# A twelve-stage decoder on one core: the order tables of four engines laid anew for all sixteen batches, with some of the PSUM banks they take

## The chip, the core and the metric

The kernel runs on one core of one Trainium2 chip. Its engines are TensorE (PE, matrix products), VectorE (DVE), ScalarE (ACT) and GpSimd (POOL); SyncE (SP) issues the DMAs. Each works through its own list of instructions in order and waits on semaphores that the others raise. The metric is the device time of one execution in microseconds (us), lower is better.

## What is computed

64 sequences of 128 tokens with 128 channels pass twelve sub-layers; each is added to its input and normalized:

```python
x = _layernorm(x + _L0_attn_ref(x, ...), axis=-1)                        # rec
x = _layernorm(x + _L0_xattn_ref(ctx_1024, x, ctx_1024, ...), axis=-1)   # x0
x = _layernorm(x + _L0_ffn_ref(x, ...), axis=-1)                         # f0, 8 routed experts
x = _layernorm(x + _L1_attn_ref(x, ...), axis=-1)                        # a1
x = _layernorm(x + _L1_xattn_ref(x, ctx_1024, ...), axis=-1)             # x1
x = _layernorm(x + _L1_ffn_ref(x, ...), axis=-1)                         # f1, fp4 rounding
x = _layernorm(x + _L2_attn_ref(x, ...), axis=-1)                        # a2
x = _layernorm(x + _L2_xattn_ref(x, ctx_1024, ...), axis=-1)             # x2
x = _layernorm(x + _L2_ffn_ref(x, ...), axis=-1)                         # f2, 6 low-rank experts
x = _layernorm(x + _L3_attn_ref(x, ...), axis=-1)                        # a3
x = _layernorm(x + _L3_xattn_ref(x, ctx_1024, ...), axis=-1)             # x3
x = _layernorm(x + _L3_ffn_ref(x, ...), axis=-1)                         # f3, attention, then 8 gated experts
return x
```

(The comments are the kernel's names of the stages.) Everything is float32. Most attentions have 16 heads of 8 channels, over 128 tokens or over a context of 77.

## The kernel before

**Opening.** Up to about 466 us the kernel prepares weights and solves the recurrence of the first layer (`opening`). It has its own table, `MEMORY_ORDER`, which the change leaves alone.

**Batches and groups.** The decoder then treats the sequences as 16 batches of four (`SEQS = 4`), called batch 0 to 15 here. Three groups (`GROUPS = 3`) each own a set of SBUF tiles, and group n works through the batches n, n+3, n+6 and so on: group 0 has six of them, the last being batch 15; group 1 ends with batch 13 and group 2 with batch 14. So three batches at different stages are in flight most of the time, and batch 15 is alone at the end.

**Steps.** For each engine a generator (`whole_tensor`, `whole_scalar`, `whole_vector`, `whole_gpsimd`) issues a batch's work in steps, one for each `yield`: 329 steps a batch on PE, 255 on ACT, 548 on DVE, 27 on POOL. The steps of one batch always come in the same order on an engine (`BATCH` lists their names). Each step ends by raising its group's semaphore, and a step that needs another engine's result waits for that semaphore's value.

**What sets the order between groups.** `ORDER` holds a string of digits for each engine: which group takes its next step. `in_order` turns it into the one list of instructions of the engine:

```python
def in_order(programs, order):

    for who in order:
        next(programs[who], None)
```

Since an engine's list is strictly in order, a step that must wait holds up everything behind it, of all groups. What hides the wait is what the table puts ahead of the waiting step.

**An attention stage** (`attention_tensor`, `attention_scalar`, `attention_vector`; x0, x1, a2, x2, a3, f3) goes through the four sequences n in a chain between engines: PE "scores n" (L1533, 16 matmuls of 32 rows), DVE four "top" reductions (L1625), PE "tops turned" (L1545), DVE "q shifted" (L1628), PE "shifted n" (L1559, 32 rows of the trace), ACT four exponentials "p n r" (L1612), and only then PE "scores n+1", since it overwrites the same banks. "out n-1" (L1582), "by tokens n-2" (L1593) and DVE's "o n-2" (L1646) follow with a lag; "shifted n" waits for "o n-2".

**The gated experts** of f3 (`gated_tensor`, `gated_scalar`, `gated_vector`) are 32 "hidden" steps (L2657, one 128x512 product), each evicted by ACT or DVE in turn (L2685, L2697), and 32 steps of an expert's second product (L2672, four 128x128 products; an expert has four), with DVE adding the result (L2704). They need only weights, so they make 64 dense steps a batch. After them come two normalizations and the store (`end_vector`, `store_sync`).

**Banks.** The eight PSUM banks are four pairs. `GIVEN` lists, as digits two by two, which group takes its next stage's pair and which pair (`give_banks`, `take_banks`); a stage's first step on PE waits for the last read by the stage that had the pair before.

**DMAs.** SP has a table of its own (`ORDER["sync"]`), which stays as it is. In it the store of batch 14 stands after the first four of the 16 weight pieces that batch 15's experts need, and ahead of the other twelve; SP waits there for batch 14's last normalization (`end normal`).

## Time and profile before

| | us |
|---|---|
| median of 3 runs | 5805.88 |
| the runs | 5800.32 to 5806.29 |
| span of the profiled execution | 5796.4 |
| PE busy in it | 4942.6 |
| DVE busy | 3559.6 |
| ACT busy | 2315.6 |
| POOL busy | 706.1 |

The profiled execution's span, from its first to its last instruction, is 9.5 us below the median of the runs, which is measured around the execution. A time of the changed kernel is therefore its span plus 9.5.
### The profile page before, as it was taken

The page shows a single profiled execution, that of the slowest core. Times are in us where ns is not written, and L with a number is a line of the kernel's source. Part 1 is how long each engine was busy: PE and PEld are TensorE (multiplying, and loading weights), DVE is VectorE, ACT ScalarE, POOL GpSimd, SP SyncE. Part 2 cuts the span into 40 slices and gives each one's busy share as a digit, 9 for nine tenths or more (in the row PEclk, how much of TensorE's full clock was granted, in tenths as well). Part 3 has the DMA queues.
Part 4 walks back from the last instruction along what each step waited for, and adds up shares of the span by engine and source line. Part 5 has one row for each costly group of instructions (what it writes and reads, how often), then busy time and mean ns, then how long its engine had stood idle before and what let it go on. Part 6 is the DMA issues. An engine that isn't in the chain of part 4 may idle for free.

```text
span 5796.4 us, 130530 instructions
## 1 busy us (share of the span) xinstructions
PE 4942.6 (85%) x55217; PEld 3576.2 (62%) x55217; DVE 3559.6 (61%) x9609; ACT 2315.6 (40%) x4634; POOL 706.1 (12%) x738
## 2 busy tenths in 40 slices
PE   5655888899898889988889989889898988988787
PEld 3544666567665666766656666666666666665554
DVE  7572576655666665657576666656656666656552
ACT  3111444434434444444543443444434344343331
POOL 6361001101101001100000110100110010110000
PEclk7576899899999999999999999999999989998897
DMA  1113000012020001110000111000020000010000
GB/s 58 25 41 100 30 13 19 3 37 61 12 63 9 23 14 32 62 39 30 31 2 28 39 41 54 16 30 18 23 67 31 30 28 13 30 41 23 1 30 26
DMA packets 144930, 184.57 MB, mean 32 GB/s; under 512 B 46074, under 2 KB 73826, under 8 KB 143714
## 3 DMA queue, kind: packets, MB, share of 16 engines
q1 hardware_dynamic: 144354, 176.23, 9.9%
q8 instruction: 442, 7.24, 0.5%
q14 instruction: 134, 1.10, 0.1%
HBM read 164.32 MB, written 11.57 MB: 30 GB/s over the span
## 4 chain that ended last, share of the span: by engine, by line
PE 69%; DVE 12%; ACT 6%; issue 3%; DMA 1%; POOL 1%; SPq 0%; POOLq 0%; DVEq 0%; ACTq 0%
PE g_bank L2672 8%; PE g_bank L2657 8%; PE g_bank L1559 7%; PE g_bank L1533 6%; PE g_bank L1582 6%; ACT g_keys_exps L1612 4%; DVE g_tops L1625 3%; PE g_bank L1503 2%; PE g_bank L2395 2%; PE g_bank L1909 2%; PE g_bank L1434 2%; PE g_bank L1919 2%; PE g_bank L1389 1%; PE g_bank L2002 1%; PE g_bank L1593 1%
## 5 line engine op out<-in xcount | busy, mean ns | idle before, releaser
L1625 DVE TENSOR_REDUCE g_tops<-g_bank 128x4 f32<-128x512 f32 (+1 forms) x1536 | 813.8, 575 | 431.1 <-PE g_bank L1533 429.5
L1612 ACT ACTIVATE g_keys_exps<-g_bank 128x512 f32<-128x512 f32 (+1 forms) x1536 | 801.7, 596 | 690.6 <-PE g_bank L1559 689.2
L1368 POOL TENSOR_TENSOR g_rstd<-g_rstd,minus_half 128x4 f32<-128x4 f32 x224 | 226.7, 1013 | 4358.1 <-DVE g_rstd L1350 4340.2
L2672 PEld LDWEIGHTS g_bank<-region,g_keys_exps 128*128 128x128 f32 x4096 | 516.9, 192 | 159.6 <-issue 144.6
L2657 PE MATMUL g_bank<-g_xT,region 128*128 128x512 f32 x1024 | 554.0, 623 | 15.3 <-DVE g_keys_exps L2697 8.4
L2672 PE MATMUL g_bank<-region,g_keys_exps 128*128 128x128 f32 x4096 | 547.4, 278 | 10.8 <-DVE g_base L2704 9.8
L1559 PE MATMUL g_bank<-g_qa,g_keys_exps 32*77 32x128 f32 (+1 forms) x12288 | 490.8, 300 | 74.4 <-DVE g_o L1646 38.3
L1559 PEld LDWEIGHTS g_bank<-g_qa,g_keys_exps 32*77 32x77 f32 (+1 forms) x12288 | 408.8, 181 | 191.7 <-issue 62.6
L1533 PE MATMUL g_bank<-g_keys_exps,g_qa 32*128 32x154 f32 (+1 forms) x6144 | 411.6, 381 | 100.3 <-ACT g_keys_exps L1612 91.9
L1582 PE MATMUL g_bank<-g_keys_exps,g_v 77*32 77x128 f32 (+1 forms) x12288 | 444.4, 289 | 60.7 <-DVE g_tops L1625 50.9
L1582 PEld LDWEIGHTS g_bank<-g_keys_exps,g_v 77*32 77x32 f32 (+1 forms) x12288 | 333.4, 115 | 176.8 <-DVE g_tops L1625 117.7
L1533 PEld LDWEIGHTS g_bank<-g_keys_exps,g_qa 32*128 32x128 f32 x6144 | 275.5, 198 | 212.3 <-ACT g_keys_exps L1612 125.3
L1606 ACT ACTIVATE g_oT_sc<-g_bank 128x256 f32<-128x256 f32 x384 | 147.5, 384 | 541.5 <-PE g_bank L1582 540.9
L2685 ACT ACTIVATE g_keys_exps<-g_bank,region 128x512 f32<-128x512 f32 x256 | 175.9, 687 | 469.0 <-PE g_bank L2657 468.7
L2697 DVE TENSOR_SCALAR g_keys_exps<-g_bank,region 128x512 f32<-128x512 f32 x256 | 191.3, 747 | 277.0 <-PE g_bank L2657 276.0
L1628 DVE TENSOR_TENSOR g_qa<-g_qa,g_bank 128x256 f32<-128x256 f32 x384 | 159.4, 415 | 189.2 <-PE g_bank L1545 186.8
L1377 ACT ACTIVATE g_x<-g_x,g_shift,g_rstd 128x128 f32<-128x128 f32 x384 | 171.4, 488 | 201.5 <-DVE g_shift L1354 201.2
L2657 PEld LDWEIGHTS g_bank<-g_xT,region 128*128 128x128 f32 x1024 | 159.5, 193 | 73.0 <-issue 61.1
L1593 PE MATMUL g_bank<-consts_sb,g_oT_sc 128*128 128x128 f32 x768 | 165.4, 300 | 30.5 <-ACT g_keys_exps L1612 17.1
L2704 DVE SCALAR_TENSOR_TENSOR g_base<-g_bank,g_gates,g_base 128x128 f32<-128x128 f32 x512 | 149.9, 341 | 53.3 <-PE g_bank L2672 46.9
L1343 DVE BATCH_NORM_STATS2 g_stats<-g_x 128x6 f32<-128x128 f32 x768 | 176.0, 279 | 3.7
L1545 PE MATMUL g_bank<-consts_sb,g_tops 128*128 128x128 f32 x384 | 119.1, 310 | 66.8 <-DVE g_tops L1625 65.7
(376 smaller groups left out, 8832.0 us busy)
## 6 DMA issues: line engine op xcount, KB each, us to landing
region<-L_w_in SPq DMA_DIRECT2D x512, 256.0 KB, 2.9
region<-xT_in SPq DMA_DIRECT2D x16, 256.0 KB, 2.7
z_scratch<-m_uT SPq DMA_DIRECT2D x1, 4096.0 KB, 11.0
g_oT_sc<-z_scratch SPq DMA_DIRECT2D x16, 256.0 KB, 3.2
g_xT<-xT_in SPq DMA_DIRECT2D x16, 256.0 KB, 3.9
g_o<-x_in SPq DMA_DIRECT2D x16, 256.0 KB, 4.1
out<-g_x SPq DMA_DIRECT2D x16, 256.0 KB, 2.3
region<-weights_in SPq DMA_DIRECT2D x1, 3020.5 KB, 10.1
```

Of the source, the lines that this page charges most:

```text
L1343: e.bn_stats(g.stats[:, n, :], src[:, n, :]).then_inc(*b.vector(f"{st} stats {n}"))
L1368: e.tensor_tensor(g.rstd[:, :], g.rstd[:, :], g.s["minus_half"], ALU.pow).then_inc(*b.gpsimd(st + " rstd"))
L1533: ins = e.matmul(bank[r][:, 2 * nk * t:2 * nk * (t + 1)].rearrange("p (i k) -> p i k", i=2), g.qa[rows, t, n, :], g.km[rows, n, t, :, 0:nk ...
L1559: ins = e.matmul(bank[r][0:nk, u * T:(u + 1) * T], g.km[rows, n, t, i, 0:nk], g.qa[rows, t, n, :], start=not masked, stop=not masked or u ...
L1582: ins = e.matmul(b.bank[st][0][32 * u:32 * u + 32, k * T:(k + 1) * T], g.v[0:nk, n, 8 * i + 4 * k + u, :], g.p[0:nk, 2 * i + k, u, :], sta ...
L1593: ins = e.transpose(b.bank[st][1][:, k * P:(k + 1) * P], outputs_of(g, n)[:, k, :], g.k["ident"])
L1612: e.activation(g.p[0:nk, r, :, :], bank[r][0:nk, :].rearrange("p (u q) -> p u q", u=4), ACT.Exp, scale=scale).then_inc(*b.scalar(f"{st} p ...
L1625: e.tensor_reduce(g.tops[:, first:first + 4].rearrange("p (t i) -> p t i", t=2), src, AX, ALU.max).then_inc(*b.vector(f"{st} top {n} {r}"))
L2657: e.matmul(bank[0][:, :], weights.part(f"w1 {x}", c), g.xT, start=True, stop=True).then_inc(*b.tensor(f"f3 hidden {k}"))
L2672: ins = e.matmul(bank[1][:, n * D:(n + 1) * D], g.gated_hid[:, x % 2, c, n * T:(n + 1) * T], weights.part(f"w2 {x}", c), start=c == n == 0 ...
L2685: e.activation(g.gated_hid[:, k // HC % 2, k % HC, :], b.bank["ex"][0][:, :], ACT.Relu, bias=g.w["f3_b1"][:, k:k + 1]).then_inc(*b.scalar( ...
L2697: e.tensor_scalar(g.gated_hid[:, x % 2, k % HC, :], b.bank["ex"][0][:, :], g.w["f3_b1"][:, k:k + 1], 0.0, ALU.add, ALU.max).then_inc(*b.ve ...
```

## The change

All four engines' strings in `ORDER` and the string `GIVEN` are replaced by others; no other line changes. Each digit occurs as often as before, so each engine issues the same steps, and each batch's steps in the same sequence: 5264 steps on PE, 4080 on ACT, 8768 on DVE, 432 on POOL. What differs is how the three groups are interleaved. The number of places where the group changes from one step to the next goes from 3623 to 3683 on PE, from 2124 to 1966 on ACT, from 4119 to 3547 on DVE and from 247 to 268 on POOL. ACT's list has 74 loads of function tables instead of 73. Of the 304 entries of `GIVEN`, 49 stages take a pair that another stage had before than until now; the others differ at most in the pair's number. (The strings are printed with other line breaks, so the code that follows stands eight lines higher: L1533 of before is L1525 after.)

```diff
 ORDER = {
     "tensor": (
-        "0000000000000000000000000000000000000000000000000000001000000111101000010100110101010011110001111001"
...
+        "00100000010001001001001000001001000001000110000000000000000000000000000000010010000010101100011110010010"
...
 GIVEN = (
-    "00010203101201130013012221132200021003110322011001132012010213102201210013011322110022211313211220020203"
...
+    "13011300100202022100131321200210020211030310221312012001010213100113002221130111222221001321132012212102"
...
```

Over most of the decoder a batch's stages begin within a few steps of where they began. Three stretches differ more.

**The start.** PE took its first step of batch 1 as its 55th and now takes it as its third; 11 steps of batch 1 now stand ahead of batch 0's experts of f0, none before. POOL began with batch 0's "rec masks" and "rec base" and now does those of batch 1 and the masks of batch 2 ahead of batch 0's masks.

**Batches 13 to 15.** On PE the last step of batch 13's experts moves from place 4882 to 4915, with 22 of its 64 expert steps now behind batch 15's "a1 y", where none stood; batch 14's "x2 y" moves from 4778 to 4832; batch 15's "x1 scores 0" moves from 4892 to 4876.

**Batches 14 and 15.** All 64 expert steps of batch 14 stood ahead of batch 15's "a3 y". Now 26 of them (11 hidden, 15 of the second product) stand between it and batch 15's own experts, among its x3 and the attention of f3. Batch 15's experts took the pair of banks that batch 14's experts had; now they take one of batch 15's own f3.

The first place in the lists is PE in the middle of the decoder, at batch 6's last attention, between "tops turned 2" (L1545) and "scores 3" (L1533, x8); L2459 and L2463 are another batch's keys and values of x3, L1389 is its turned x. Before:

```order
L1545 MATMUL g_bank<-consts_sb,g_tops 128x128
L2146 MATMUL g_bank<-f_upT,g_keys_exps 128x352
L2459 MATMUL g_bank<-g_ctxT,region 128x308
L2463 MATMUL g_bank<-region,g_ctxT 77x128 x4
L1559 MATMUL g_bank<-g_qa,g_keys_exps 128x128 x16
L1533 MATMUL g_bank<-g_keys_exps,g_qa 128x256 x8
L1389 MATMUL g_bank<-consts_sb,g_x 128x128 x4
```

And after:

```order
L1537 MATMUL g_bank<-consts_sb,g_tops 128x128
L2138 MATMUL g_bank<-f_upT,g_keys_exps 128x352
L1551 MATMUL g_bank<-g_qa,g_keys_exps 128x128 x16
L2451 MATMUL g_bank<-g_ctxT,region 128x308
L2455 MATMUL g_bank<-region,g_ctxT 77x128 x4
L1381 MATMUL g_bank<-consts_sb,g_x 128x128 x4
L1525 MATMUL g_bank<-g_keys_exps,g_qa 128x256 x8
```

The three steps of the other batch moved from beside the pair "shifted 2" and "scores 3" to between them.

The second place is PE at the end, the last attention of batch 15. Before, from "scores 0" to the second "shifted":

```order
L1533 MATMUL g_bank<-g_keys_exps,g_qa 128x256 x8
L1545 MATMUL g_bank<-consts_sb,g_tops 128x128
L1559 MATMUL g_bank<-g_qa,g_keys_exps 128x128 x16
L1533 MATMUL g_bank<-g_keys_exps,g_qa 128x256 x8
L1582 MATMUL g_bank<-g_keys_exps,g_v 32x128 x16
L1545 MATMUL g_bank<-consts_sb,g_tops 128x128
L1559 MATMUL g_bank<-g_qa,g_keys_exps 128x128 x16
```

And after, the same stretch:

```order
L1525 MATMUL g_bank<-g_keys_exps,g_qa 128x256 x8
L2664 MATMUL g_bank<-region,g_keys_exps 128x128 x4
L2649 MATMUL g_bank<-g_xT,region 128x512
L2664 MATMUL g_bank<-region,g_keys_exps 128x128 x4
L1537 MATMUL g_bank<-consts_sb,g_tops 128x128
L1551 MATMUL g_bank<-g_qa,g_keys_exps 128x128 x16
L2649 MATMUL g_bank<-g_xT,region 128x512
L2664 MATMUL g_bank<-region,g_keys_exps 128x128 x4
L1525 MATMUL g_bank<-g_keys_exps,g_qa 128x256 x8
L2649 MATMUL g_bank<-g_xT,region 128x512
L1574 MATMUL g_bank<-g_keys_exps,g_v 32x128 x16
L2664 MATMUL g_bank<-region,g_keys_exps 128x128 x4
```

Steps of batch 14's experts (L2649 and L2664, which were L2657 and L2672) came between.

The third place is DVE where batch 15's own experts begin; g0 tiles are batch 15's, g2 tiles batch 14's. L2622 (now L2614) adds the second bias, L2697 (now L2689) evicts a hidden product. Before:

```order
L1862 TENSOR_TENSOR g0_gates<-g0_small 128x32
L2622 TENSOR_TENSOR g0_base<-g0_base,g_bank3 128x512
L2697 TENSOR_SCALAR g0_keys_exps<-g_bank2,region 128x512 x4
L2704 SCALAR_TENSOR_TENSOR g0_base<-g_bank3,g0_gates,g0_base 128x128 x4
L2697 TENSOR_SCALAR g0_keys_exps<-g_bank2,region 128x512 x2
```

And after:

```order
L2614 TENSOR_TENSOR g0_base<-g0_base,g_bank3 128x512
L2696 SCALAR_TENSOR_TENSOR g2_base<-g_bank7,g2_gates,g2_base 128x128
L1335 BN_STATS g2_stats<-g2_base 128x6 x4
...
L2689 TENSOR_SCALAR g0_keys_exps<-g_bank2,region 128x512
L1346 SCALAR_TENSOR_TENSOR g2_shift<-g2_mean_var,g2_rstd 128x4
...
L2713 TENSOR_TENSOR g2_x<-g2_x,g2_o 128x512
L2689 TENSOR_SCALAR g0_keys_exps<-g_bank2,region 128x512
L1335 BN_STATS g2_stats<-g2_x 128x6 x4
...
L1351 TENSOR_SCALAR g2_x<-g2_x,g2_mean_var,g2_rstd 128x128
L2689 TENSOR_SCALAR g0_keys_exps<-g_bank2,region 128x512
```

Batch 14's two closing normalizations, which stood among batch 15's stages a3 and x3, now stand between batch 15's first evictions.

## Rows read from the trace of the kernel before

**Rows 1.** The page: span, busy time of each engine, and the chain by engine.

```profile
span 5796.4 us, 130530 instructions
...
PE 4942.6 (85%) x55217; PEld 3576.2 (62%) x55217; DVE 3559.6 (61%) x9609; ACT 2315.6 (40%) x4634; POOL 706.1 (12%) x738
...
PE 69%; DVE 12%; ACT 6%; issue 3%; DMA 1%; POOL 1%; SPq 0%; POOLq 0%; DVEq 0%; ACTq 0%
```

**Rows 2.** Windows: length, busy us (instructions) of PE, PEld, DVE, ACT, POOL; then PEclk.

```profile
470.00:490.00 20.00, 12.65 (x58) 7.16 (x58) 7.93 (x20) 4.65 (x8) 11.11 (x15) 0.82 0.58 192
490.00:540.00 50.00, 29.82 (x340) 21.96 (x340) 12.70 (x41) 11.79 (x24) 1.03 (x1) 0.51 0.01 1
540.00:647.00 107.00, 83.03 (x868) 61.49 (x871) 53.91 (x140) 38.07 (x71) 7.49 (x7) 0.91 0.13 40
830.00:5190.00 4360.00, 3904.68 (x44005) 2827.32 (x44003) 2775.15 (x7589) 1901.20 (x3626) 400.33 (x368) 0.95 0.10 30
5198.00:5281.00 83.00, 82.83 (x651) 63.03 (x650) 47.67 (x104) 22.11 (x39) 1.56 (x2) 1.00 0.17 55
5281.00:5443.00 162.00, 123.80 (x1267) 82.59 (x1265) 95.57 (x262) 62.12 (x119) 14.44 (x13) 0.78 0.02 4
5509.00:5614.00 105.00, 100.98 (x784) 71.83 (x784) 54.55 (x131) 34.04 (x60) 7.54 (x6) 0.97 0.12 39
5614.00:5708.00 94.00, 56.88 (x440) 37.75 (x438) 32.46 (x110) 22.04 (x43) 8.36 (x8) 0.61 0.02 6
```

**Rows 3.** Timeline (start, us, what, idle before) of PE: batch 6 waits.

```profile
3050.63 1.17 PE L1559 MATMUL g_bank<-g_qa,g_keys_exps 32*128 32x128 f32 x32 [1.48 <-DVE g_o L1646]
3054.65 2.09 PE L1533 MATMUL g_bank<-g_keys_exps,g_qa 32*128 32x256 f32 x16 [2.85 <-ACT g_keys_exps L1612]
```

**Rows 4.** Timeline of all engines at the decoder's start, batch 0.

```profile
469.10 0.51 SPq L2909 DMA_DIRECT2D g_o<-x_in  x1
...
471.38 1.04 POOL L1760 TENSOR_TENSOR g_keys_exps<-consts_sb,g_kq_dot 128x512 f32<-128x512 f32 x1
...
475.55 0.69 DVE L1734 TENSOR_TENSOR g_keys_exps<-g_bank,g_keys_exps 128x512 f32<-128x512 f32 x1 [2.88 <-PE g_bank L1694]
```

**Rows 5.** Timeline of PE, last attention of batch 15, alone.

```profile
5645.26 1.15 PE L1533 MATMUL g_bank<-g_keys_exps,g_qa 32*128 32x256 f32 x16 [0.90 <-issue]
...
5691.39 0.79 PE L1662 MATMUL g_bank<-region,g_oT_sc 128*128 128x128 f32 x2 [0.69 <-ACT g_oT_sc L1673]
```

**Rows 6.** Timeline of PE, attention a3 of batch 15 with batch 14's experts between.

```profile
5567.48 1.15 PE L1533 MATMUL g_bank<-g_keys_exps,g_qa 32*128 32x256 f32 x16
...
5575.11 1.02 PE L2657 MATMUL g_bank<-g_xT,region 128*128 128x512 f32 x2
...
5577.07 1.10 PE L2657 MATMUL g_bank<-g_xT,region 128*128 128x512 f32 x2
...
5613.51 1.06 PE L1662 MATMUL g_bank<-region,g_oT_sc 128*128 128x128 f32 x8
```

**Rows 7.** The same view, two attentions side by side.

```profile
5440.28 1.15 PE L1533 MATMUL g_bank<-g_keys_exps,g_qa 32*128 32x256 f32 x16
...
5448.46 1.15 PE L1533 MATMUL g_bank<-g_keys_exps,g_qa 32*128 32x256 f32 x16 [1.15 <-ACT g_keys_exps L1612]
```

**Rows 8.** DMA issues: KB each, median us from issue to landing.

```profile
region<-L_w_in SPq DMA_DIRECT2D x512, 256.0 KB, 2.9
...
g_o<-x_in SPq DMA_DIRECT2D x16, 256.0 KB, 4.1
```

**Rows 9.** Timeline of all engines: batch 15's experts begin, and the end.

```profile
5708.16 2.08 PE L2657 MATMUL g_bank<-g_xT,region 128*128 128x512 f32 x2
...
5730.83 1.13 PE L2672 MATMUL g_bank<-region,g_keys_exps 128*128 128x128 f32 x8 [0.17 <-DVE g_base L2704]
...
5783.81 1.13 DVE L2704 SCALAR_TENSOR_TENSOR g_base<-g_bank,g_gates,g_base 128x128 f32<-128x128 f32 x4 [3.99 <-PE g_bank L2672]
...
5793.65 0.40 SPq L2918 DMA_DIRECT2D out<-g_x  x1
```

More of the change, by code:

```diff
@@ new lines @@
+        "01011201200012101122102202222002202212002201022022120001010110101021022020221010202101212121020101120010"
+        "01220021011122011221201102201101022021020001011010001101020102011012212001010112010121112102012112202102"
+        "12220121012122201121121012200000101101202210021210211022021000010201010212110101201011021022010100001102"
+        "12000112100100212001002020120121001002021002200200002101002211001200020012200120000102000200100221202000"
+        "12112121211122121211122212001102012210201002002201221020110120010122102112112021001201121020112112111211"
@@ new lines @@
+    "gpsimd": (
+        "11200001010201021120021201001200000120010121111101000211210000002121102022221211101122101022221012202222"
+        "01021200000021012012110111010021120010002010112202222121110112211021222010221222202102012000100120101111"
+        "01211200100200210000110220222221111101220121022210010222221201022000012001010210111010211210100002012112"
+        "00202222211111120121021202210221222020212000001200101201011101102121010000002121100202222220102201022220"
+        "0000000000002200"),
```

377 lines of the change are left out of this document (180 added, 197 removed).

## The prediction, as it was made before the result

> **What bounds the kernel now.** I read the page first, then windows, then the timeline of PE at a few places. The page [rows 1] names PE: 4942.6 of 5796.4 us busy, and 69% of the chain that ended last lies on PE, 12% on DVE, 6% on ACT. The change cannot alter the busy time as such, since the same steps are issued; it can only alter the idle time of PE, and how long a matmul takes where the clock is at its lower level.
>
> The windows [rows 2] show where both are. In the middle, from 830 to 5190 us, PE is busy 3904.7 of 4360 us, idle 455 us (10%), at a mean clock of 0.95. At the decoder's start, from 470 to 540 us, batch 0 is alone: busy 12.65 + 29.82 of 70 us, idle 27.5, and from 490 us the clock is 0.51, which is its 1.2 GHz level nearly throughout. From 5198 to 5281 us the experts of batch 13 fill PE entirely (82.8 of 83), and then two batches in attention leave it idle for 38.2 of 162 us at clock 0.78. From 5509 to 5614 us batch 14's experts fill it again (idle 4.0 of 105), and from 5614 to 5708 us batch 15 is alone: idle 37.1 of 94 us at clock 0.61. So dense, undemanding work is piled up just ahead of stretches that lack it, three times.
>
> A typical idle piece of the middle is at 3054.65 us [rows 3]: "scores 3" of batch 6 stands directly behind "shifted 2", needs four exponentials on ACT between, and PE waits 2.85 us; the step ahead of it had waited 1.48 us for DVE.
>
> **Part 1, the middle: -27 us.** In the order after, three steps of another batch stand in that gap. I counted such places in both orders: for each step on PE that waits for a chain through other engines, how much PE work stands between it and the step that began the chain, at each step's median duration in the trace, against the quick tenth of the delays that the trace shows for that pair of steps. Of the steps in the middle, 846 had too little cover before and 690 have too little after; the missing cover adds up to 692 us and 610 us, 12% less. That sum is larger than the 455 us of idle time since one wait covers several shortages. Both ends: if PE's idle time shrinks in proportion, 0.12 x 455 = 54 us; if what is gained at one place is waited for at the next, nothing, and DVE's list can make it worse. Counting there how often a step stands behind one whose PE result comes over 5 us of PE work later, I find 437 places before and 484 after. I take half of the proportion, 27 us, since one count speaks for and one against. ACT's additional table load is nothing on an engine that is busy 40% [rows 1]. Bank pairs taken from another stage are part of the same count only where they hold a step back; I price them at nothing, since no wait for a bank stands out in the trace.
>
> **Part 2, the start: -6 us.** Eleven steps of batch 1, about 12 us of PE work, come ahead of batch 0's experts of f0. They fill the 27.5 us that PE is idle there and leave the 107 us that follow, where PE is busy 83 [rows 2]. The gain is between nothing (batch 0's chain sets that stretch) and 12; I take 7. Against it stands POOL's new order. Batch 0's masks ran at 471.38 us and DVE used them at 475.55 [rows 4]. Now batch 1's base comes first, whose load is issued at 469.10 and lands 4.1 us later after 0.5 of issue [rows 4, 8], at about 473.7; then three POOL steps of 1.04 us end batch 0's masks at 476.8. DVE's step and all of batch 0 behind it come 1.3 us later. Together -6.
>
> **Part 3, batches 13 to 15: -14 us.** 22 expert steps of batch 13 move from the stretch that is full to the one that is idle for 38.2 us [rows 2]. A hidden and a second product take 5577.07 - 5575.11 = 1.96 us together [rows 6], 0.98 each, so 21.6 us of work move. Where PE is full a step removed is a gain; where they go, they can hide in idle time or push the attention chains. Between nothing and 21.6, plus what a higher clock than 0.78 returns; I take 14, two thirds, since batch 14 gives way meanwhile (its "x2 y" stands 54 steps later) and has to catch up.
>
> **Part 4, the end: -19 us.** Batch 14's experts had cost 64 x 0.98 = 63 us of the 105 us up to "a3 y". Now 26 steps, 25.5 us, come after it, and 3 earlier.
> - Up to batch 15's "a3 scores 0" 13 steps fewer stand among f2 and the projections, less the 3 that come ahead: 10 x 0.98 = 9.8 us off a stretch with hardly any idle time. I take 9.
> - The attention a3 took 5613.51 - 5567.48 = 46.0 us with 30 expert steps inside [rows 6]. With 14 it is bound by its own chain. Alone and at the low clock the attention of f3 takes 5691.39 - 5645.26 = 46.1 us [rows 5]; at full clock one sequence of it takes 5448.46 - 5440.28 = 8.2 us [rows 7], four 33 us and some 5 for the lag. So between 0 and 8; PE is then still busy enough to be at its higher level, and I take 8.
> - The attention of f3 gets 15 steps. The same ends, 0 and 8; since each filler delays the chain by part of itself, I take 4.
> - On DVE batch 14's end stands between batch 15's first evictions. That chain takes 5793.65 - 5783.81 = 9.8 us alone [rows 9]. Eight hidden steps and the first expert take batch 15 from 5708.16 to 5730.83, 22.7 us [rows 9], so most of it is hidden. Behind it SP waits with twelve weight pieces: begun with the second bias, the chain with four evictions of 0.7 us and waits between ends about 15 us later, the first piece lands 0.4 + 2.9 us [rows 8, 9] after that, at 19 of 22.7 us. Between 0 and 5; I take 2 lost.
>
> Sum: -27 - 6 - 14 - 19 = -66 us. The span becomes 5796.4 - 66 = 5730.4, and with the 9.5 us around it **5740 us**, 1.1% below the median of 5805.9.
>
> **The clock, weighed apart.** In the trace the clock follows how busy PE is: 0.51 with PE busy 60%, 0.61 at 61%, 0.78 at 76%, 0.97 at 96% [rows 2]. The Trainium skill (TensorE: Matmul & The Clock Gate, "Part 1: The HAM clock gate") says that the throttled 1.2 GHz is the default state and that activity releases it, with no level between the two. By that rule the filler would buy more than the idle time that it fills, which is the first rival below; the trace agrees as far as these shares go, and no row shows a stretch of one attention with this much filler.
>
> **Rivals.**
> - The filler lifts the clock in all the lonely stretches. From 490 to 540 us 29.8 us of busy time would halve, of which about 10 lie on the chain; at the end the attention of f3 would gain its full 8 and the steps after it some 4. -66 - 10 - 8 = -84: 5722 us.
> - The middle gains in proportion: -93, 5713 us. For it: the count of short covers falls by 18%. Against: DVE's count.
> - The middle gives nothing: each local swap only moves the wait. -39: 5767 us. For it: no stage of the middle begins more than a few steps elsewhere.
> - The filler is not free either: attention with it takes the 46 us that it takes without [rows 5, 6], and batch 14's end holds up batch 15. Only the 9 us of part 4 and the start are left, -15 + 5 = about -10: 5796 us, no measurable change.
> - Slower, by DVE's list. DVE is in order and is used 61% [rows 1]; its longer runs of one group (3547 changes for 4119) keep a ready result of another group waiting. The 47 additional places each hold DVE for 5 us or more. If each lets PE run dry for 1.1 us, which is the small wait in [rows 7] with 1.15, that is 52 us; with the middle's gain gone the sum is -39 + 52 = +13: 5819 us. It decides from 36 places on (39 / 1.1). Against it: PE has other groups' steps in hand at most of them.
> - That the change does nothing is excluded: the orders differ at thousands of places.
>
> **How the numbers follow.** Chances: 5740 0.38; clock 0.17 (5722); middle in full 0.10 (5713); middle nothing 0.20 (5767); only crumbs 0.07 (5796); slower 0.08 (5819). The first four are faster by over 0.2%, 11.6 us, about what a measurement of this kernel can tell from no change: 0.85; the fifth is the same, 0.07; the last slower, 0.08. The range leaves out the slower case, most of the fifth and the lowest tenth of the low side: 5695 to 5798, where 5695 is the clock and the proportional middle together, -84 - 27 = -111. The likeliest case's own range is 5722 to 5758.
>
> **What would show it.** Windows of the changed kernel: the start should show PE busy more than 42.5 of its first 70 us; the middle, from batch 0's x2 to batch 15's f0, should show idle time of about 430 us instead of 455; the stretch after batch 15's "a1 y" less than 20% idle time at a clock above 0.78; the time from batch 15's "a3 y" to its second bias (94 us before) should stay near 90 with PE busy over 75%; and its a3 attention should take under 40 us instead of 46. Wrong it would be if the waits of PE for DVE grow in the middle, if PE waits for a weight load in batch 15's experts, or if that attention keeps its 46 us.

## The result, and the profile after

| | before | after |
|---|---|---|
| median (us) | 5805.91 | 5463.65 |
| its runs | 5800.32 to 5806.29 | 5458.81 to 5466.28 |
| ratio, 95% interval | | 0.9417 [0.9403, 0.9432] |
| span of the profiled execution | 5796.4 | 5464.1 |
| PE busy / idle in it | 4942.6 / 853.8 | 4782.4 / 681.7 |

The change makes the kernel 5.8% faster. (Two executions of all in this document, of 14.2 and 15.5 ms, one of the kernel before and one of e15, count in no ratio.) The forecast was 1.1%, with 5695 us as the lowest time of its range. The page after, where [rows 1] stood before:

```profile
span 5464.1 us, 130532 instructions
...
PE 4782.4 (88%) x55217; PEld 3486.1 (64%) x55217; DVE 3585.9 (66%) x9609; ACT 2303.5 (42%) x4635; POOL 705.7 (13%) x738
PEclk7676899999999999999999999999999999999998
...
PE 63%; DVE 12%; issue 7%; ACT 6%; POOL 1%; DMA 1%; SPq 1%; POOLq 0%; DVEq 0%; ACTq 0%
```

The span is 332.3 us shorter, and only 172.1 us of it are idle time of PE. The other 160.2 us are busy time: the same 55217 matmuls took less. The row of granted clocks, in 40 slices, gives a first hint. After, one of the last nine slices is under 9; before, four were:

```profile
PEclk7576899899999999999999999999999989998897
```

The windows after (columns as in [rows 2]) are the start, the middle from batch 0's x2 to batch 15's f0, the stretch with batches 14 and 15 in attention, and the end up to batch 15's second bias in two pieces.

```profile
470.00:490.00 20.00, 13.50 (x74) 8.43 (x72) 7.96 (x25) 5.33 (x9) 10.55 (x15) 0.91 0.57 183
490.00:540.00 50.00, 32.03 (x381) 22.16 (x381) 20.95 (x73) 15.77 (x33) 3.09 (x3) 0.71 0.00 1
815.90:4874.10 4058.20, 3759.43 (x43823) 2749.55 (x43824) 2792.62 (x7571) 1881.53 (x3609) 401.91 (x369) 0.98 0.11 32
4984.00:5142.00 158.00, 125.41 (x1375) 84.35 (x1374) 97.43 (x249) 62.33 (x119) 12.45 (x11) 0.87 0.03 10
5203.00:5296.00 93.00, 78.52 (x645) 52.16 (x644) 47.56 (x113) 32.20 (x59) 7.66 (x7) 0.97 0.10 29
5296.00:5376.00 80.00, 63.66 (x578) 43.63 (x577) 34.64 (x101) 23.50 (x44) 6.30 (x6) 0.96 0.07 21
```

The middle before, cut at the same two steps of PE, is this row:

```profile
825.40:5166.80 4341.40, 3884.58 (x43819) 2812.41 (x43819) 2766.76 (x7563) 1890.89 (x3607) 401.58 (x369) 0.95 0.10 30
```

It took 4341 us and takes 4058, 283 us less. Idle time fell from 457 to 299 us (158), busy time by 125. The view rounds the clock to two digits; the clock records of the two traces themselves have TensorE at its lower level for 413 us of the middle before and for 188 us after, with PE busy in 363 and 161 us of that. Sixteen products of "scores" take 2.09 us at the lower level and 1.15 at the higher, so the 202 us of busy time that moved to the higher level account, as an estimate, for 90 to 100 of the 125 us. What the rest is, is not shown.

How the lead grew, by the start of the same PE step in both timelines:

| step | before | after | lead | gained since |
|---|---|---|---|---|
| batch 0, f0 logits | 538.4 | 532.7 | 5.7 | 5.7 |
| batch 0, x2 scores 0 | 825.4 | 815.9 | 9.5 | 3.8 |
| batch 3, f3 conv | 2006.0 | 1934.8 | 71.2 | 61.7 |
| batch 6, f3 conv | 3009.7 | 2868.6 | 141.1 | 69.9 |
| batch 9, f3 conv | 3893.9 | 3693.4 | 200.5 | 59.4 |
| batch 15, f0 logits | 5166.8 | 4874.1 | 292.7 | 92.2 |
| batch 15, f2 logits | 5509.5 | 5208.7 | 300.8 | 8.1 |
| batch 15, a3 scores 0 | 5567.5 | 5256.3 | 311.2 | 10.4 |
| batch 15, a3 y | 5613.5 | 5295.1 | 318.4 | 7.2 |
| batch 15, f3 second bias | 5706.2 | 5375.2 | 331.0 | 12.6 |
| end of the span | 5796.4 | 5464.1 | 332.3 | 1.3 |

The lead grows all through the middle, by 50 to 70 us per 1000 us, and 283 of the 332 us come from there. What PE waits for in the middle, by the step that waited (us in total, times, longest), before:

```profile
PE g_bank L1533 <- ACT g_keys_exps L1612: 66.0, 64, 2.8
PE g_bank L1545 <- DVE g_tops L1625: 43.0, 46, 3.3
PE g_bank L1582 <- DVE g_tops L1625: 37.8, 64, 1.8
PE g_bank L1559 <- DVE g_o L1646: 30.5, 33, 1.8
PE g_bank L1559 <- DVE g_qa L1628: 26.2, 37, 2.6
```

and after, the same five, with one that grew (the load of x transposed, 12.0 us before):

```profile
PE g_bank L1525 <- ACT g_keys_exps L1604: 49.0, 60, 2.7
PE g_bank L1537 <- DVE g_tops L1617: 34.2, 49, 2.3
PE g_bank L1678 <- DMA g_xT<-xT_in: 30.9, 10, 4.4
PE g_bank L1574 <- DVE g_tops L1617: 16.9, 27, 2.0
PE g_bank L1551 <- DVE g_o L1638: 15.5, 20, 2.7
...
PE g_bank L1551 <- DVE g_qa L1620: 12.8, 21, 1.6
```

All five links of the attention chain fell, from 203.5 to 128.4 us together. None vanished and no single place stands out. The place of [rows 3], batch 6's last attention, is in the timeline of PE after:

```profile
2905.68 1.17 PE L1551 MATMUL g_bank<-g_qa,g_keys_exps 32*128 32x128 f32 x32 [1.77 <-DVE g_o L1638]
2906.78 1.02 PE L2451 MATMUL g_bank<-g_ctxT,region 128*128 128x308 f32 x2
2907.60 1.92 PE L2455 MATMUL g_bank<-region,g_ctxT 128*77 128x128 f32 x8
2909.66 0.45 PE L1381 MATMUL g_bank<-consts_sb,g_x 128*128 128x128 f32 x1
2910.63 0.90 PE L1381 MATMUL g_bank<-consts_sb,g_x 128*128 128x128 f32 x3 [0.52 <-DVE g_x L1351]
2911.46 2.09 PE L1525 MATMUL g_bank<-g_keys_exps,g_qa 32*128 32x256 f32 x16
```

The three steps of batch 7 between "shifted 2" and "scores 3" cover the exponentials; the wait of 2.85 us is gone, 0.52 us of another kind came in. (The 16 matmuls of "scores" took 2.09 us here against 1.15 elsewhere: by the clock records this one ran at the lower level.)

### The profile page after: what moved, and what is told of

Read it like the earlier page. It is cut to its first block, busy times and chain, and to the rows that moved or that the text cites. A ratio compares the mean times of both kernels' runs of the same rounds, so it can differ in the third digit from the quotient of the medians.

```text
span 5464.1 us, 130532 instructions
## 1 busy us (share of the span) xinstructions
PE 4782.4 (88%) x55217; PEld 3486.1 (64%) x55217; DVE 3585.9 (66%) x9609; ACT 2303.5 (42%) x4635; POOL 705.7 (13%) x738
## 4 chain that ended last, share of the span: by engine, by line
PE 63%; DVE 12%; issue 7%; ACT 6%; POOL 1%; DMA 1%; SPq 1%; POOLq 0%; DVEq 0%; ACTq 0%
PE g_bank L2649 8%; PE g_bank L2664 8%; PE g_bank L1551 6%; PE g_bank L1574 5%; PE g_bank L1525 4%; ACT g_keys_exps L1604 4%; DVE g_tops L1617 3%; PE g_bank L1495 2%; PE g_bank L1901 2%; PE g_bank L1911 2%; PE g_bank L2387 2%; PE g_bank L1426 2%; PE g_bank L1381 1%; PE g_bank L1994 1%; PE g_bank L2249 1%
## 5 line engine op out<-in xcount | busy, mean ns | idle before, releaser
L2664 PEld LDWEIGHTS g_bank<-region,g_keys_exps 128*128 128x128 f32 x4096 | 517.3, 192 | 151.4 <-issue 140.6
L2649 PE MATMUL g_bank<-g_xT,region 128*128 128x512 f32 x1024 | 550.7, 619 | 8.6 <-DVE g_keys_exps L2689 4.2
L2664 PE MATMUL g_bank<-region,g_keys_exps 128*128 128x128 f32 x4096 | 546.4, 278 | 3.7 <-DVE g_base L2696 3.7
L1551 PE MATMUL g_bank<-g_qa,g_keys_exps 32*77 32x128 f32 (+1 forms) x12288 | 455.8, 285 | 53.7 <-DVE g_o L1638 34.2
L1551 PEld LDWEIGHTS g_bank<-g_qa,g_keys_exps 32*77 32x77 f32 (+1 forms) x12288 | 379.8, 169 | 158.8 <-DVE g_o L1638 57.0
L1574 PE MATMUL g_bank<-g_keys_exps,g_v 77*32 77x128 f32 (+1 forms) x12288 | 430.7, 283 | 39.7 <-DVE g_tops L1617 28.9
L1525 PE MATMUL g_bank<-g_keys_exps,g_qa 32*128 32x154 f32 (+1 forms) x6144 | 389.3, 365 | 77.3 <-ACT g_keys_exps L1604 67.4
L1525 PEld LDWEIGHTS g_bank<-g_keys_exps,g_qa 32*128 32x128 f32 x6144 | 262.1, 189 | 190.5 <-ACT g_keys_exps L1604 112.1
L2689 DVE TENSOR_SCALAR g_keys_exps<-g_bank,region 128x512 f32<-128x512 f32 x256 | 191.5, 748 | 241.5 <-PE g_bank L2649 240.3
L2649 PEld LDWEIGHTS g_bank<-g_xT,region 128*128 128x128 f32 x1024 | 158.5, 192 | 59.2 <-issue 45.7
L1635 DVE RECIPROCAL g_total<-g_bank 128x16 f32<-128x16 f32 x384 | 95.9, 250 | 131.7 <-PE g_bank L1585 131.0
```

What stands on the lines that cost most here:

```text
L1525: ins = e.matmul(bank[r][:, 2 * nk * t:2 * nk * (t + 1)].rearrange("p (i k) -> p i k", i=2), g.qa[rows, t, n, :], g.km[rows, n, t, :, 0:nk ...
L1551: ins = e.matmul(bank[r][0:nk, u * T:(u + 1) * T], g.km[rows, n, t, i, 0:nk], g.qa[rows, t, n, :], start=not masked, stop=not masked or u ...
L1574: ins = e.matmul(b.bank[st][0][32 * u:32 * u + 32, k * T:(k + 1) * T], g.v[0:nk, n, 8 * i + 4 * k + u, :], g.p[0:nk, 2 * i + k, u, :], sta ...
L2649: e.matmul(bank[0][:, :], weights.part(f"w1 {x}", c), g.xT, start=True, stop=True).then_inc(*b.tensor(f"f3 hidden {k}"))
L2664: ins = e.matmul(bank[1][:, n * D:(n + 1) * D], g.gated_hid[:, x % 2, c, n * T:(n + 1) * T], weights.part(f"w2 {x}", c), start=c == n == 0 ...
L2689: e.tensor_scalar(g.gated_hid[:, x % 2, k % HC, :], b.bank["ex"][0][:, :], g.w["f3_b1"][:, k:k + 1], 0.0, ALU.add, ALU.max).then_inc(*b.ve ...
```

## The experiments

All ratios are to the kernel before, run on the same chip as the experiment (median 5788.7 to 5795.7 us there). Where a gain over the kernel before is given in us, it is the ratio times 5806. Where a run is compared with the changed kernel, its time stands against 5464 us, measured on another chip; as the kernel before was 10 to 17 us quicker on the experiments' chips, such differences are good to some 15 us. Orders are compared digit by digit; of each string one place is shown.

### Where in the decoder the gain lies

Three kernels take over one stretch of the new tables each, at cuts where both orders have issued the same steps. (At the cuts the bank pairs are numbered anew, so that each stage finds the pair that its table means.)

```diff
 # e1: tensor (2088 digits differ), scalar 1272, vector 3291, gpsimd 127, from 825 us on, to 5090 us
-"0100200020200101122011000211011220200202202222122020202220120122000010110110102102022012201202010121"
+"0100200022000101120120001210112210220222200220221200220102202212000101011010102102202022101020210121"
...
 # e2: tensor 64, scalar 53, vector 90, gpsimd 12, up to 700 us
-"0000000000000000000000000000000000000000000000000000001000000111101000010100110101010011110001111001"
+"0010000001000100100100100000100100000100011000000000000000000000000000000001001000001010110001111001"
...
 # e3: tensor 263, scalar 188, vector 436, gpsimd 18, from 5090 us on
-"1020021001001010020022022102012001100201020011020002212212122122112212212121001202102010012010012122"
+"1020021001001010020022022102012001100201020011020002212212122122112212212111002021022001100210102122"
```

> All five tables are those of before up to the beginning of batch 0's last x2 attention (825 us of the trace of before) and from batch 15's first steps on (5090 us); between them stands the changed order, with its banks. The traces of before and after differ by 290 us between batch 0's x2 and batch 15's first steps. Theory A (the gain is made place by place in the middle): 5806 - 280 = 5526 us, with 5510 to 5545. Rival B (the new start shifts the three groups against each other and the middle gains by that): under 60 us of gain, 5750 us or more. Rival C (start, middle and end only fit together): slower than before.

Measured: 5524.55 us, ratio 0.9520 [0.9495, 0.9545], 278 us less.

> Only the order up to 700 us of the changed kernel's trace (batches 0 to 2 up to their first stages) is the new one, the rest is that of before. Theory A: the 8 us by which batch 0's x1 and f1 come earlier in the changed kernel, 5798 us, with 5790 to 5806. Rival B (the start's shift is what makes the middle faster): 5600 us or less.

Measured: 5783.81 us, ratio 0.9975 [0.9954, 0.9996], 14 us less, with 12 us of uncertainty.

> Only the order from batch 15's first steps on (5090 us of the trace of before) is the new one. In the changed kernel the lead grows from 303 us at batch 15's x1 to 332 us at the end, and 10 us of the lead before that belong to batches 13 and 14 in this stretch. Theory A: 5806 - 35 = 5771 us, with 5760 to 5780; the forecast's own two parts for it were 14 and 19 us, 33 together. Rival: under 10 us, 5796 us or more, if the end's gain needs the middle's order.

Measured: 5755.56 us, ratio 0.9927 [0.9904, 0.9951], 42 us less, 28 to 56.

The three gains add up to 334 us, with some 20 of uncertainty, against 342 measured for the whole. So within that the stretches are independent of each other. The middle is won in the middle and not by the start's shift, and start and end gave what the forecast said of them, or somewhat more.

### What idle time costs beside itself

Two kernels add to the changed one, at the second "shifted" of each of the 96 attentions, either work or idleness on PE:

```diff
         if n:
             e.wait_ge(*b.scalar[f"{st} oT {n - 1}"])
         if n > 1:
             e.wait_ge(*b.vector[f"{st} o {n - 2}"])
+        if n == 1:                                                       # e7
+            for k in range(8):
+                e.matmul(bank[k % 4][:, 0:P], g.k["ident"], g.k["ident"], start=True, stop=True)
...
+        if n == 1:                                                       # e8
+            for k in range(40):
+                e.wait_ge(g.fixed, 6)
```

> The changed kernel with eight more 128x128 products of constants on TensorE ahead of the second 'shifted' of each of the 96 attentions, 8 x 0.28 = 2.2 us each by the 278 ns of the trace, 215 us in all; their results are overwritten. It is one half of a pair with the next. Theory K (idle time costs the clock beside itself): the clock stays at 0.94 or above, the time rises by up to 215 us, 5600 to 5680. Rival (the clock does not answer to such pieces): the pair is equal per us of TensorE's time that is added.

> The changed kernel with 40 waits that are long fulfilled at the same 96 places instead of the eight products, so that TensorE is idle there; how long is read from the trace (estimate: 1 to 3 us each, 100 to 290 us in all). Theory K: the clock falls below that of e7, by 0.03 or more, and the time rises by clearly more than the idle time added, a fifth more or so. Rival (no answer of the clock): the same mean clock as e7, and the time rises by the idle time added or less.

The pages of e7:

```profile
span 5629.9 us, 133604 instructions
...
PE 4973.2 (88%) x56753; PEld 3676.1 (65%) x56753; DVE 3584.6 (64%) x9609; ACT 2302.8 (41%) x4635; POOL 705.5 (13%) x738
```

and of e8, with the first row of its waits of PE:

```profile
span 5617.0 us, 132452 instructions
...
PE 4854.1 (86%) x55217; PEld 3539.5 (63%) x55217; DVE 3585.6 (64%) x9609; ACT 2304.1 (41%) x4635; POOL 705.9 (13%) x738
```

```profile
PE g_bank L1554 <- issue: 90.3, 69, 2.1
```

Both pages count the opening too, and its share of idle time changes from run to run though its steps and its length do not: PE was busy in 256.6 of the first 466 us in the changed kernel, in 267.6 in e8 and in 304.2 in e9. So the pair is read from 466 us on, here the changed kernel and then e8:

```profile
466.00:5464.10 4998.10, 4525.78 (x51520) 3289.32 (x51520) 3289.26 (x8912) 2210.30 (x4233) 474.61 (x446) 0.96 0.11 32
```

```profile
466.00:5617.00 5151.00, 4586.49 (x51520) 3335.33 (x51520) 3288.96 (x8912) 2210.80 (x4233) 476.62 (x450) 0.95 0.10 31
```

Work added, e7: the span rose by 165.8 us, busy time from 466 us on by 171.7, idle time there fell by 5.8, and the mean clock was 0.941 as in the changed kernel (0.940). Idleness added, e8: the number of matmuls is the same, yet beside 92.2 us more idle time there were 60.7 us more busy time; the span rose by 152.9 and the mean clock fell to 0.927. So one us of idle time cost 1.66 us, 0.66 of it in slower matmuls. The clock fell by less than the 0.03 that I had expected; the price per us came out above the fifth that I had set as a mark. The Trainium skill (TensorE: Matmul & The Clock Gate, "HAM oscillation — how this bites in real kernels") describes a kernel whose waits for DMA between bursts of matmuls throw the clock back, so that they are paid a second time in slower matmuls. This pair agrees, with its 60.7 us; the waits that the page tells of last 3 to 5 us, and here the longest added one was 2.1 us.

The same sum, from 466 us on, for the other kernels of this document, each against the one that it was made from: for each us by which idle time changed, busy time changed with it by 0.36 us in e5, 0.53 in e6, 0.60 in e10, 0.61 in e12, 0.66 between e16 and e17, 0.72 in e13 and 1.11 in e14; for the change itself, in the middle, by 0.79. The price is not one number, but in none of them is it nothing.

### Which lists carry it

```diff
 # e9: against before; GIVEN alone
-    "00010203101201130013012221132200021003110322011001132012010213102201210013011322110022211313211220020203"
+    "13011300100202022100131321200210020211030310221312012001010213100113002221130111222221001321132012212102"
...
 # e4: against before; tensor alone, in the middle, 2060 digits
-"0100200020200101122011000211011220200202202222122020202220120122000010110110102102022012201202010121"
+"0100200022000101120120001210112210220222200220221200220102202212000101011010102102202022101020210121"
...
 # e5: against before; scalar 716 digits, vector 2545, gpsimd 116; here scalar
-"0000000000000000000000000000000000000000000000001000110011011100111111100111111010111110011000001010"
+"0000000000000000000000000000000000000000000000001000110110011100111111111001111100111110011000000110"
...
 # e6 and e10: against after; vector 2983 digits (e6 also scalar 876, gpsimd 166)
-"0000000000000000000000011111000100111111111110000000000100000000000000000000000000000000000000000000"
+"0100000000000000000000010111111100001011111110000000100000000000000000000000011110000000000000000000"
```

> All orders are those of before; only GIVEN is the changed one, by which 49 of 304 stages take a bank pair that another stage had before. Theory A (as the forecast had it, the banks cost and gain nothing): within 0.3% of before. Rival (the banks hold steps back where the orders do not suit them, or free them): 30 us or more away from it on either side.

Measured: 5795.89 us, ratio 1.0010 [0.9993, 1.0027]. The banks give nothing, as forecast.

> In the middle TensorE takes its steps in the changed order, while ScalarE, VectorE, GpSimd and the banks keep theirs of before; where a step could never come because another engine's list has a step of another group first, the first possible one of the changed order is taken (265 of some 4400 steps). Theory P (the cover that stands between a step on TensorE and the chain that it waits for is what counts): a good part of the 290 us, 5600 to 5700 us. Theory F (the four lists have to agree, and TensorE's alone makes it wait for VectorE): slower than before, over 5850 us. Theory V (VectorE's order makes the gain): within 1% of 5806 us.

Measured: 6692.74 us, ratio 1.1536 [1.1507, 1.1564]. TensorE's new order (as far as the other lists let it be taken) under the old lists of the others is 15% slower, with 1421.1 us of idle time on PE where the kernel before has 853.8. The lists can't be judged one by one in this way.

> TensorE's order and the banks are those of before; the lists of ScalarE, VectorE and GpSimd are sorted by when each step's inputs were there in the trace of before, so that none stands behind one that became ready later (VectorE's group changes fall from 4119 to 2957). Theory V (what the change gains comes from the side engines' order, in which a ready step no longer stands behind one that waits): well over 50 us of gain, 5700 us or less. Theory P+fit (TensorE's order carries it, and the other lists only have to agree with it): 5806 us within 30 either way. Rival (the side lists of before hold back uncritical steps on purpose, and first come, first served loses that): slower, 5840 us or more.

> The same with the changed kernel: TensorE's order and banks are the new ones, the lists of the other three are sorted by when their inputs were there in its own trace. Theory V: most of the gain is lost or something more is won, away from 5464 us by over 50. Theory P+fit: within 30 us of 5464. Rival (uncritical steps held back on purpose): 5500 us or more, and e5 slower by as much.

> The changed kernel with VectorE's list alone sorted by when the inputs of its steps were there, where e6 sorted three lists and lost 314 us (5778). Theory V1 (what counts on the side engines is which of several ready steps VectorE, the busiest of them, takes first): most of the 314 us, 5680 us or more. Rival V2 (ScalarE, with the exponentials that 'scores' waits for, carries it): under 100 us lost, 5560 us or less.

Measured: e5 6033.2 us, ratio 1.0401 [1.0345, 1.0458]; e6 5777.69 us, 0.9970 [0.9948, 0.9993]; e10 5688.46 us, 0.9833 [0.9802, 0.9864].

| side engines' lists | PE's order and banks of before | new ones |
|---|---|---|
| as in that kernel | 5793 | 5464 |
| sorted by arrival | 6033 | 5778 |

Read down: side lists sorted by arrival lose 240 us before and 314 after, and 225 of the 314 with VectorE's list alone. Read across: with side lists made by one and the same rule, TensorE's order and the banks are worth 255 us (the banks nothing, by e9, which tried them under the old orders). By this one way of splitting the 329 us, some three quarters come with TensorE's order, and the rest with how well the side lists fit it. Theory V falls, and with it the reading that taking ready steps first on VectorE is a gain. Why the sorted lists lose is not shown: the rival's reason, that the tables hold back uncritical steps on purpose, is one, and that any change to lists that fit each other costs time, as in e4, is another.

### Whether a wait can be mended at its place

```diff
 # e11: against after; tensor, 44 ready steps moved ahead of a waiting one (102 digits)
-"2002110202012210012021122211012211020111120100010021012110010110001110100010111010001010110100011200"
+"2002110202012210012021122201112211200112110100010021012110010110001110100010111010001010110100012100"
...
 # e12: against after; tensor, 210 "scores" one place earlier (412 digits)
-"2002100022000101120120001210112210220222200220221200220102202212000101011010102102202022101020210121"
+"2002100020200101102120001210112201220222200220221200220102202212000100111010012102200222101020120121"
...
 # e13: against after; tensor, 254 "scores" one place later (508 digits)
-"2002100022000101120120001210112210220222200220221200220102202212000101011010102102202022101020210121"
+"2002100022000101121020001210112212020222200220221200220102202212000101101010120102202202101020201121"
...
 # e14: against before; tensor, 54 waiting "scores" one place later (108 digits)
-"2121021010010020010021212112121012212101012200111022020200010110001010110022102110120100221010110101"
+"2121021010010020010022112112121012212101012200111022022000010110001010110022102110120100221010110101"
```

> The changed kernel with TensorE's order changed at 44 places between 700 and 5200 us: where TensorE waits over 0.3 us in the trace and the next step of another group has its inputs already, that step is moved ahead of the waiting one. The waits that it can fill add up to 27 us. Theory A (each us of idle filled is won, and the clock adds its 0.9): 5464 - 50 = 5414 us, with 5405 to 5440. Rival (filled waits only move, since the moved step delays the chain that it stands before): within 0.2% of 5464.

Measured: 5468.26 us, ratio 0.9445 [0.9424, 0.9467], no gain on the changed kernel. From 466 us on PE is idle for 467.6 us instead of 472.3: of the 27 us of waits that could be filled nearly all came back elsewhere.

> The changed kernel with 210 of the 284 steps 'scores 1', 'scores 2' and 'scores 3' of the middle one place earlier on TensorE, ahead of another group's step of about 1 us; nothing else moves. By the slack that the trace shows at these places, 90 us of waits would appear. Theory A (the cover ahead of a chain's step is what the table gives): idle time up by 90 us, and the clock makes it 150 to 170, 5610 to 5640 us. Rival (slack elsewhere and the earlier start of the next chain give it back): under 50 us, 5515 us or less.

Measured: 5706.9 us, ratio 0.9859 [0.9835, 0.9884], 243 us slower than the changed kernel's 5464, 1.2 us for each step moved. Its page and the row that answers to "scores" (L1540 here, 67.4 us at 82 places in the changed kernel):

```profile
span 5699.0 us, 130532 instructions
...
PE 4886.7 (86%) x55217; PEld 3539.9 (62%) x55217; DVE 3583.6 (63%) x9609; ACT 2303.8 (40%) x4635; POOL 706.3 (12%) x738
```

```profile
PE g_bank L1540 <- ACT g_keys_exps L1619: 147.4, 168, 2.7
```

The 90 us of new waits that I had read from the slack became 146.2 us of idle time (from 466 us on), and busy time rose by another 88.7 us there: the idle time is 1.6 times what the cover is short by, and the slower matmuls add 0.6 for each us of it. (Over the whole span, with the opening, it is 130.6 and 104.3 us.)

> The counterpart of e12: the changed kernel with 254 of its 'scores 1' to 'scores 3' in the middle one place later on TensorE, behind another group's step of about 1 us. Theory A (cover ahead of a chain's step is what was short): the 51 us of waits that stand at these steps vanish, and the clock adds to it, 5464 - 50 = 5414 us or a little above. Theory B (an attention chain that is served a step later costs as much as one that is served a step too early; the table holds both in balance): slower by over 100 us, 5560 us or more. Rival: the two cancel, within 30 us of 5464.

Measured: 5836.63 us, ratio 1.0076 [1.0048, 1.0103], 372 us slower than the changed kernel, 1.5 us for each step. Its waits, "out" (L1589) and "tops turned" (L1552), which had been 28.9 and 41.1 us in the changed kernel:

```profile
PE g_bank L1589 <- DVE g_tops L1632: 107.0, 152, 3.1
PE g_bank L1552 <- DVE g_tops L1632: 67.9, 77, 2.9
```

"scores", the link that was given more cover, waited 31.4 us instead of 67.4.

> The kernel before, with the 54 'scores' of the middle that wait over 0.3 us in its trace (55 us of waits together) one place later, behind the next group's step. Theory A (the cover was short at such places and moving one step mends it): a gain of 55 us and as much again by the clock less 31 us for which the moved step would wait itself, 5806 - 50 = 5756 us. Theory B (a wait can't be mended at its own place, since a step put there is held up itself or holds up the chain): within 15 us of before, or slower.

Measured: 5898.14 us, ratio 1.0180 [1.0156, 1.0204]: 105 us slower than before, 1.9 us for each of the 54 steps. Its waits, where the kernel before had 65.7 us at "tops turned", 50.9 at "out" and 91.9 at "scores" over its whole run:

```profile
PE g_bank L1552 <- DVE g_tops L1632: 82.1, 67, 3.6
PE g_bank L1589 <- DVE g_tops L1632: 72.2, 108, 2.1
...
PE g_bank L1540 <- ACT g_keys_exps L1619: 54.1, 43, 2.6
```

"scores" waited 37.8 us less, as meant, and the two links behind it 37.7 us more. The step that was put ahead of "scores" is the one that had covered the reductions between "scores" and "tops turned". From 466 us on idle time rose by 48.1 us and busy time by 53.5. Theory B holds in e13 and e14, one in either kernel: cover added at one link is missing at the next. e11 says that filled waits come back, and e12 that the opposite move costs as well.

### A wait taken away without moving a step

The changed kernel's table of SyncE has a batch's next loads behind its store, which waits for the last normalization:

```diff
+    done = None
     for b in batches:
-        yield from loads_sync(e, b, dram, b.index * SEQS)
-        yield from store_sync(e, b, dram, b.index * SEQS)
+        loads = loads_sync(e, b, dram, b.index * SEQS)
+        for _ in range(5):
+            next(loads)
+            yield
+        if done:
+            yield from store_sync(e, done, dram, done.index * SEQS)
+        yield from loads
+        done = b
+    yield from store_sync(e, done, dram, done.index * SEQS)
```

> The changed kernel, in which SyncE issues a group's next loads (masks, dots, context, z and x transposed) ahead of the store of its last batch instead of behind it; only the load of x itself stays behind the store. In the changed kernel's trace TensorE waits 30.9 us at 10 places of the middle for x transposed, which SyncE issues 2.2 us after a store that it had waited 13 us for. Theory A: these waits vanish and the clock adds its 0.8 of it, 5464 - 31 - 25 = 5408 us, with 5400 to 5435. Theory B (as e11 to e14, a wait that is taken away at one place comes back behind it, since the lists are laid for it): within 12 us of 5464.

Measured: 5444.45 us, ratio 0.9402 [0.9386, 0.9418], between the two theories, and too near to the changed kernel's own interval on another chip. So both ran side by side:

> The changed kernel itself, on one chip with the next run, as its measure: ratio to before 0.9417 within 0.0015, if the chips agree.

> The kernel of e15 again, beside the changed kernel on the same chip. In e15's trace the ten waits of the middle for x transposed are down to three short ones, 26 us less with the start's; Theory A: 26 + 21 of the clock, 5464 - 47 = 5417 us or a ratio of 0.9336. Theory B (part of it comes back behind): between a tenth and a half of it, ratio 0.939 to 0.941.

Measured: the changed kernel 5469.82 us (5463.29 to 5480.42), ratio 0.9439 [0.9412, 0.9467]; with the loads ahead 5442.97 us (5427.07 to 5444.22), ratio 0.9386 [0.9362, 0.9411]. That is 27 us less, and no run of the one reaches the other. The changed kernel's own ratio came out 0.0022 above the 0.9417 of the first measurement, a little more than I had allowed. The gain lies between the theories: over half of the 47 us that theory A foresaw, so part of the wait did come back, or was not worth its 1.8. The load of x transposed in SyncE's queue, batch 9, in the changed kernel and then in e15's:

```profile
3050.70 0.40 SPq L2910 DMA_DIRECT2D out<-g_x  x1
...
3052.88 0.43 SPq L2897 DMA_DIRECT2D g_xT<-xT_in  x1
```

```profile
3027.46 0.43 SPq L2897 DMA_DIRECT2D g_xT<-xT_in  x1
3038.37 0.40 SPq L2910 DMA_DIRECT2D out<-g_x  x1
```

TensorE's waits for these loads over the whole run are 47.5 us at 11 places in e16, and in e17:

```profile
PE g_bank L1678 <- DMA g_xT<-xT_in: 22.3, 4, 18.6
```

25 us of waits gone; idle time fell by 26.1 us and busy time by 18.7 in the profiled pair, 44.8 together, against 27 us in the medians. The profiled run of e17 is the quickest of its five, at a mean clock of 0.944 where the others had 0.937 to 0.941, so part of the 18.7 us is chance. This version is faster than both kernels, 6.1% under the kernel before.

## Why the prediction was wrong, point by point

**Part 1, the middle, -27: this is the step that failed.** It measured -283 in the traces (158 us of idle time and 125 us of busy time) and -278 in e1. That TensorE's idle time would shrink by better cover was right; the size was not, and three things in it were wrong.

- *The clock was left out of the middle.* The prediction weighed it "apart" and gave it only to the lonely stretches, since 0.95 looked like full speed. Every us of idle time saved there brought 0.79 us of busy time with it (125 for 158), and e8, where idleness alone was added, shows 0.66. So the term has to be multiplied by 1.7 to 1.8.
- *The difference was turned into a proportion.* The count found 82 us less missing cover (692 to 610). I scaled it to 12% of the idle time, 54 us, on the ground that one wait covers several shortages. In e12 it was the other way round: 90 us of shortage made 146.2 us of idle time and 88.7 of busy time, 2.6 us for each. 82 x 2.6 = 214 us would have been nearer, yet still 69 short; it is worked out afterwards, and only e12 stands behind the factor.
- *It was halved on the word of a count that these runs do not bear out.* VectorE's steps behind a later one were read as harm. e6 and e10 sorted such steps out of the changed kernel's lists and lost 314 and 225 us.

The forecast had idle time of about 430 us in the middle, and "Wrong it would be if the waits of PE for DVE grow". Idle time was 299 us, and those waits fell, from 137.5 to 79.4 us over the four rows above.

**The rival "slower, by DVE's list"** fell with the result, and so did "the middle gives nothing", of which I had written that no stage begins more than a few steps elsewhere. "The middle gains in proportion", 5713 us, priced the idle time at a third of what it was. In e13, one place for 254 steps was worth 372 us. How far steps move says nothing of what it is worth.

**Part 2, the start, -6:** right, 5.7 us at batch 0's f0, and 14 with 12 of uncertainty in e2. PE is busy 45.5 of the first 70 us (42.5 before), as named. Its clock there rose as well, from 0.51 to 0.71.

**Part 3, batches 13 to 15, -14:** too high, 8.1 us between batch 15's f0 and f2. The stretch is idle for 20.6% of its time (32.6 of 158) at clock 0.87; under 20% and over 0.78 were named.

**Part 4, the end, -19:** 31.5 us. By its steps: up to "a3 scores 0" 10.4 (forecast 9); attention a3 7.2, it takes 38.8 us instead of 46.0 (forecast 8); f3's attention 41.2 instead of 46.1, 4.9 (forecast 4); the rest of x3 and f3 7.7 in all where nothing was foreseen; behind it 1.3 won where 2 lost were forecast, and no wait for a weight piece stands in batch 15's experts. From "a3 y" to the second bias it takes 80 us where I had said 90, with PE busy 80%. The surplus goes with the clock again: 0.61 before [rows 2], 0.96 after. The first rival, the clock in the lonely stretches, is what happened here; e3's 42 us (28 to 56) against 33 doesn't contradict it.

**The range.** It ended at 5695 because its lowest case was the sum of two rivals that both priced idle time one to one in the middle. Also the 9.5 us "around the span": the profiled execution after was itself timed at 5466.3 us, 2.2 us more than its span, so most of the 9.5 must have been the difference between one run and the median.

**What stays open.** e1 to e3 show where, e4 to e10 which lists, e8 and e12 the price. What distinguishes the new order of the middle is not shown: PE's waits over 0.25 us in it went from 512 to 345, and moving steps by one place at the waits that the trace shows gave nothing (e11) or lost (e14). In both tables such moves lead nowhere better; why the new one as a whole has shorter waits was not found.

## What to carry to other kernels

Price idle time of TensorE at clearly more than its length where the granted clock of the stretch is under 1, even at 0.95, since part of what is saved comes back as faster matmuls: here mostly at 1.5 to 1.8 times, with 1.4 and 2.1 as the ends. Take such prices from the stretch that the edit touches, not from a page that holds other stretches too. Where several in-order lists are interlaced, a step moved by one place cost more than a step's time in three of four trials, so a table laid anew can be worth far more than a count of its differences says, and neither list can be judged alone. A wait that comes from outside the lists, such as a load queued behind a store, could be taken away by itself, for over half of what it seemed to be worth, and is worth looking for first.

## What the runs showed of the hardware

The clock fell although the waits were short: in the middle before, no wait of PE was over 3.8 us, and 438 of the 583 over 0.15 us were under 1 us; by the clock records it went down to the lower level 69 times, for 413 of 4341 us. With 35% less idle time it did so 32 times, for 188 of 4058 us. Of the products of "shifted" with 32x128 operands in the changed kernel, 5115 of 5886 at the higher level took 270 ns and 183 of 232 at the lower one took 416. The view has both levels in one row (count, then duration min/median/max in ns):

```profile
L1551 PE MATMUL g_bank<-g_qa,g_keys_exps x12288: 266/270/578, 490.0 to 5355.3; 32*77 32x128 f32 x104, 32*128 32x128 f32 x95
```

Waits that are long fulfilled cost TensorE time as well: 40 of them before a step left it idle for 90.3 us at 69 places in e8, 1.3 us each.
